# Feed forward of a gated block: output passes and transposes of the inner values, singly or in groups of two

## The chip, the cores and the metric

The kernel runs on one core of one Trainium2 chip. The metric is device microseconds from start to end of one execution, the median of several runs. The core has five engines with queues of their own: PE (TensorE: matmuls and transposes, with the weight loads shown apart as PEld), DVE (VectorE), ACT (ScalarE), POOL (GpSimd) and SP (SyncE, here only transfers). They meet through semaphores; each engine takes its own instructions strictly in the order in which they are written.

## The reference

The block is a cross attention (32 heads) with a gate, followed by a sparse feed forward with a gate. The change lies in the feed forward alone. Its mathematics, cut from the reference:

```python
xf = x.reshape(B * T, M)                      # 2048 rows of 512, after a layer norm
inter = xf @ c1_w.T @ c2_w.T                  # low rank selector, 1792 values a row
blk = inter.reshape(B * T, n_blocks, SPARSITY)  # 56 blocks of 32
idx = jnp.argmax(blk, axis=-1) + jnp.arange(0, INTER, SPARSITY)
h = jax.nn.relu(jnp.einsum('bkm,bm->bk', w1[idx], xf))
out = jnp.einsum('bk,bkm->bm', h, w2t[idx])
```

The result is x + tanh(g_ffn) * out.

## The kernel before

The first 1600 us of the program are the projections and the attention; they are not touched. The feed forward takes the rows in 16 tiles of 128 (`PAIRS` is 16; a tile is called j below). Instead of gathering, the kernel computes all 1792 inner values of a tile, multiplies them by a mask that keeps one in each block, turns them round, and multiplies by all of w2. Every product of full accuracy is three matmuls (`three`, lines 1345 to 1347), since each operand is held as a rounded part "hi" and a remainder "lo".

PE's steps, by the functions of the program:

- `hidden(t, k)`: inner values of tile t, column group k. Groups 0 to 2 have 512 columns, group 3 has 256. 12 matmuls a group.
- `selector(t, k)`: the selector values, one matmul a group (L1512).
- `transpose_h(t, k)`: turns round group k of the masked inner values (`h_picked`): 4 transposes of 128x128 for groups 0 to 2, 2 for group 3 (L1535).
- `output(t, k)`: adds group k to the tile's output: 12 matmuls for groups 0 to 2, 6 for group 3.
- `f_transpose_x(t)`: turns round the normalised input of tile t, 4 transposes (L1491), and `low_rank(u)`: the first selector product for two tiles, 12 matmuls of 256 columns. Both are done for two later tiles at once, in the tiles for which `prep` is true: j = 2, 4, 6, 8, 10, 12. These are called preparing tiles here.

PE writes tile j's stage as follows: output of tile j-1 and transposes of tile j in turns, then (preparing tiles) `low_rank`, then `hidden(j+1, k)` and `selector(j+2, k)` in turns.

What is transposed goes on in two steps: ACT copies the bank to `h_picked_t_hi` (`ht_hi`, L900), DVE computes `h_picked_t_lo` from the bank and that copy (`ht_lo`, L1241), and only then is the bank free. The two banks 4 and 5 serve all `transpose_h` groups in turn, and of the two `f_transpose_x` of a preparing tile the second: the list `ffn_uses` hands them out, in the order T0, T1, x(j+3), T2, T3 (T0 to T3 are the four groups of `transpose_h(j, .)`; x(j+2) goes to bank 7). So x(j+3) waits until `ht_lo` of T0 is done, T2 until `ht_lo` of T1 is, T3 until `xft_lo` of x(j+3) is. `output` accumulates in bank 6, `hidden` uses 0 and 1, `selector` 2 and 3.

DVE's own order, which is written by hand too, is for a tile j: `ht_lo(j,0)`, `ht_lo(j,1)`, in preparing tiles `fx_lo(j+2)` and `fx_lo(j+3)` (L1180), `block_rank(j+1)` (L1216, after POOL's `rank`, L701), `ht_lo(j,2)`, `first_max(j+1)` (L1222), `ht_lo(j,3)`, in preparing tiles `low_rank` (L1192 and L1194), `finish(j-1)` (L1246), then four times `pick_h(j+1,k)` (L1232) and `block_max(j+2,k)` (L1203), and at last `mark_max(j+2)` (L1211). `selector(j+2,0)` needs DVE's `low_rank`; `hidden(j+1,2)` needs bank 0, which `pick_h(j+1,0)` frees.

Of the kernel before, what the change touches and what calls it, by code (L numbers as in the profile page):

```python
# [112 lines left out]
def build(nc, x, ctx_t, bias, mask, gates, wq, wk, wv, wo, c1, c2, w1, w2, out):  # L113
# [17 lines left out]
    with ExitStack() as whole:  # L131
# [206 lines left out]
        def job_raw(r):  # L338
            _, is_v, i = JOBS[r]
            return vraw[i % 2] if is_v else kraw[i % 2]  # L340

        def job_dest(r):
            _, is_v, i = JOBS[r]
            return vw[i // 8][i % 2] if is_v else kw[i % 2]

        def job_raw_in(r):
            _, is_v, i = JOBS[r]
            return loaded(vraw_in if is_v else kraw_in, i)
# [59 lines left out]
        def split_done(n):  # L408
            return lo_sem[PIECES[n][5]], pieces_to(n, 5)

        def bank_free(use):
            b = f_before[use]
            if b is None:
                bk = f_bank[use]
                return (dve_s, dve_s, act_pt, act_pt, dve_clo, dve_clo, dve_wo, dve_wo)[bk], SLOTS
            if b[0] in ("x", "t", "out"):
                return {"x": dve_fx, "t": dve_ft, "out": dve_o}[b[0]], b[1] + 1
            return {"sel": act_i, "h": dve_hm, "ht": dve_hl}[b[0]], 4 * b[1] + b[2] + 1
# [924 lines left out]
        def _(pe):  # L1343
            def three(o, a, b, first_mm, last_mm, grouped=True):
                pe.matmul(o, a[0], b[0], start=first_mm, stop=False, skip_group_check=not grouped)  # L1345
                pe.matmul(o, a[0], b[1], start=False, stop=False, skip_group_check=not grouped)  # L1346
                return pe.matmul(o, a[1], b[0], start=False, stop=last_mm, skip_group_check=not grouped)  # L1347

            def hi_lo(ts_, *idx):
                return [t[idx] for t in ts_]  # L1350
# [136 lines left out]
            def f_transpose_x(t):  # L1487
                pe.wait_ge(*bank_free(("x", t)))
                pe.wait_ge(dve_xn, LN + t + 1)
                for c in range(CH):  # L1490
                    mm = pe.transpose(bank[f_bank[("x", t)]][:, c * P:(c + 1) * P],  # L1491
                                      fxn[t % 2][:, c * P:(c + 1) * P], ident[:, :])
                mm.then_inc(pe_x, 1)

            def low_rank(u):
                pe.wait_ge(*bank_free(("t", u)))
                pe.wait_ge(dve_fx, 2 * u + 2)
                if u == 0:
                    pe.wait_ge(*split_done(piece_no[("c1", 0)]))
                for c in range(CH):  # L1500
                    mm = three(bank[f_bank[("t", u)]][:, 0:FU], hi_lo(c1s, full, c, full),
                               hi_lo(xft[u % 2], full, c, full), c == 0, c == CH - 1)
                mm.then_inc(pe_t, 1)

            def selector(t, k):
                u, a = divmod(t, 2)
                pe.wait_ge(*bank_free(("sel", t, k)))
                pe.wait_ge(dve_ft, u + 1)
                if t == 0 and k == 0:
                    pe.wait_ge(*split_done(piece_no[("c2", 1)]))  # L1510
                c0, w = IB[k]
                pe.matmul(bank[f_bank[("sel", t, k)]][:, 0:w], ts[u % 2][:, a * P:(a + 1) * P],  # L1512
                          c2s[:, c0:c0 + w], start=True, stop=True).then_inc(pe_i, 1)

            def hidden(t, k):
                u, a = divmod(t, 2)
                c0, w = IB[k]
                pe.wait_ge(*bank_free(("h", t, k)))
                pe.wait_ge(dve_fx, t + 1)
                if t == 0:  # L1520
                    for n in range(c0 * CH // PIECE, (c0 + w) * CH // PIECE):
                        pe.wait_ge(*split_done(piece_no[("w1", n)]))
                for c in range(CH):
                    col = c0 * CH + c * w
                    mm = three(bank[f_bank[("h", t, k)]][:, 0:w],
                               hi_lo(xft[u % 2], full, c, slice(a * P, (a + 1) * P)),
                               hi_lo(w1s, full, slice(col, col + w)), c == 0, c == CH - 1)
                mm.then_inc(pe_h, 1)

            def transpose_h(t, k):  # L1530
                a, w = TGRP[k]
                pe.wait_ge(*bank_free(("ht", t, k)))
                pe.wait_ge(dve_hm, 4 * t + k + 1)
                for c in range(a, a + w):
                    mm = pe.transpose(bank[f_bank[("ht", t, k)]][:, (c - a) * P:(c - a + 1) * P],  # L1535
                                      hm[:, c * P:(c + 1) * P], ident[:, :])
                mm.then_inc(pe_ht, 1)

            def output(t, k):
                a, w = TGRP[k]  # L1540
                if k == 0:
                    pe.wait_ge(*bank_free(("out", t)))
                pe.wait_ge(dve_hl, 4 * t + k + 1)
                if t == 0:
                    for n in range(a // 2, (a + w + 1) // 2):
                        pe.wait_ge(*split_done(piece_no[("w2", n)]))
                for c in range(a, a + w):
                    o = (c % 2) * D
                    mm = three(bank[f_bank[("out", t)]][:, :], hi_lo(hmt, full, c, full),
                               hi_lo(w2s[c // 2], full, slice(o, o + D)), c == 0, c == IC - 1)  # L1550
                mm.then_inc(pe_ou, 1)
# [28 lines left out]
            hidden(0, 3)  # L1580
            for j in range(PAIRS):
                prep = j % 2 == 0 and j + 3 < PAIRS
                for k in range(4):
                    if j:
                        output(j - 1, k)
                    transpose_h(j, k)
                    if j and prep and k == 1:
                        f_transpose_x(j + 2)
                        f_transpose_x(j + 3)
                if prep:  # L1590
                    low_rank(j // 2 + 1)
                for k in range(4):
                    if j + 1 < PAIRS:
                        hidden(j + 1, k)
                    if j + 2 < PAIRS:
                        selector(j + 2, k)
# [58 lines left out]
```

## Time and profile before

| | us |
|---|---|
| median of 3 runs | 1982.55 |
| lowest and highest | 1980.14, 1984.99 |
| profiled execution | 1984.87 |
| its span | 1982.8 |
| PE busy in the span | 1932.2 |
| feed forward, from about 1600 to the end | 383 |

The span is the time from the first to the last instruction of the profiled execution; what lies around it is 2.07 us. A difference of about 0.2% (4 us) is what timed runs of this kernel tell from none. Start times in the rows are microseconds from the span's start. A matmul's duration overlaps the next one's, so the length of a stretch of PE's work is read from start to start.

### The profile page before, as it was taken

The page shows a single profiled execution, that of the slowest core. Times are in us where ns is not written, and L with a number is a line of the kernel's source. Part 1 is how long each engine was busy: PE and PEld are TensorE (multiplying, and loading weights), DVE is VectorE, ACT ScalarE, POOL GpSimd, SP SyncE. Part 2 cuts the span into 40 slices and gives each one's busy share as a digit, 9 for nine tenths or more (in the row PEclk, how much of TensorE's full clock was granted, in tenths as well). Part 3 has the DMA queues.
Part 4 walks back from the last instruction along what each step waited for, and adds up shares of the span by engine and source line. Part 5 has one row for each costly group of instructions (what it writes and reads, how often), then busy time and mean ns, then how long its engine had stood idle before and what let it go on. Part 6 is the DMA issues. An engine that isn't in the chain of part 4 may idle for free. (4 is left out here: it accounts for less than half of the span.)

```text
span 1982.8 us, 32380 instructions
## 1 busy us (share of the span) xinstructions
PE 1932.2 (97%) x12220; PEld 1675.9 (85%) x12220; DVE 1077.1 (54%) x1748; ACT 769.4 (39%) x1963; POOL 972.0 (49%) x772
## 2 busy tenths in 40 slices
PE   7999999999999999999899999999999869999999
PEld 5999988899988888888788888888888757888887
DVE  5343465333355553334366656765656676676773
ACT  3233333322233333333356555656565532222221
POOL 6766688766688787787322222223222342122110
PEclk8999999999999999999899999999999989999999
DMA  3555665554454554577597767888766331000000
GB/s 121 190 190 168 194 207 190 187 169 150 151 189 172 190 188 172 175 257 230 219 250 255 213 198 272 256 222 271 218 180 186 123 114 54 22 22 22 22 22 17
DMA packets 185578, 329.54 MB, mean 166 GB/s; under 512 B 11856, under 2 KB 118480, under 8 KB 176464
## 3 DMA queue, kind: packets, MB, share of 16 engines
q1 hardware_dynamic: 185424, 327.47, 51.6%
q8 instruction: 99, 1.62, 0.3%
q14 instruction: 55, 0.45, 0.1%
HBM read 214.17 MB, written 113.25 MB: 165 GB/s over the span
## 5 line engine op out<-in xcount | busy, mean ns | idle before, releaser
L1345 PE MATMUL bank<-tokens_hi,wkq_hi 128*128 128x512 f32 x896 | 352.4, 393 | 12.5 <-DVE tokens_lo L979 10.9
L1346 PE MATMUL bank<-tokens_lo,wkq_hi 128*128 128x512 f32 x896 | 351.1, 392 | 0.0
L1347 PE MATMUL bank<-tokens_hi,wkq_lo 128*128 128x512 f32 x896 | 351.1, 392 | 0.0
L664 POOL TENSOR_TENSOR wkq_lo<-raw_wkq,wkq_hi 128x768 fp32r<-128x768 f32 (+1 forms) x128 | 287.8, 2268 | 124.5 <-ACT wkq_hi L773 124.3
L1345 PE MATMUL bank<-wv_s_hi,tokens_hi 128*128 128x256 f32 x896 | 254.3, 284 | 1.5 <-POOL wv_s_lo L664 1.5
L1347 PE MATMUL bank<-wv_s_hi,tokens_lo 128*128 128x256 f32 x896 | 253.5, 283 | 0.0
L1346 PE MATMUL bank<-wv_s_lo,tokens_hi 128*128 128x256 f32 x896 | 253.5, 283 | 0.0
L687 POOL TENSOR_TENSOR bias_mask<-bias_in,mask_add 128x256 f32<-128x256 f32 x128 | 87.5, 684 | 308.2 <-DVE scores L1117 308.2
L1345 PE MATMUL bank<-wo_hi,attn_t_hi 128*128 128x512 f32 x512 | 213.7, 417 | 0.0
L1345 PEld LDWEIGHTS bank<-tokens_hi,wkq_hi 128*128 128x128 f32 x896 | 169.6, 189 | 50.4 <-DVE tokens_lo L979 11.9
L1347 PE MATMUL bank<-wo_hi,attn_t_lo 128*128 128x512 f32 x512 | 201.8, 394 | 0.0
L1346 PE MATMUL bank<-wo_lo,attn_t_hi 128*128 128x512 f32 x512 | 200.2, 391 | 0.0
L1347 PEld LDWEIGHTS bank<-tokens_hi,wkq_lo 128*128 128x128 f32 x896 | 169.5, 189 | 35.6
L1346 PEld LDWEIGHTS bank<-tokens_lo,wkq_hi 128*128 128x128 f32 x896 | 169.6, 189 | 34.7
L857 ACT ACTIVATE probs_t<-bank 64x256 f32<-64x256 f32 x256 | 96.7, 378 | 238.4 <-PE bank L1453 237.0
L791 ACT ACTIVATE p<-bank 128x512 f32<-128x512 f32 x96 | 57.4, 598 | 316.5 <-PE bank L1347 316.5
L844 ACT ACTIVATE exp<-scores,negmax 128x64 f32<-128x64 f32 x512 | 172.0, 337 | 10.8 <-DVE negmax L1121 7.5
L664 POOL TENSOR_TENSOR wv_s_lo<-raw_wv,wv_s_hi 128x1536 fp32r<-128x1536 f32 (+1 forms) x32 | 130.1, 4066 | 89.8 <-ACT wv_s_hi L773 89.8
L1345 PEld LDWEIGHTS bank<-wv_s_hi,tokens_hi 128*128 128x128 f32 x896 | 171.9, 192 | 2.1 <-POOL wv_s_lo L664 1.9
L999 DVE TENSOR_TENSOR c<-bank,u 128x512 f32<-128x512 f32 x96 | 66.4, 692 | 196.1 <-PE bank L1347 196.1
L1346 PEld LDWEIGHTS bank<-wv_s_lo,tokens_hi 128*128 128x128 f32 x896 | 172.0, 192 | 0.2
L1347 PEld LDWEIGHTS bank<-wv_s_hi,tokens_lo 128*128 128x128 f32 x896 | 171.9, 192 | 0.0
(115 smaller groups left out, 3910.9 us busy)
## 6 DMA issues: line engine op xcount, KB each, us to landing
k_t<-c SPq DMA_DIRECT2D x128, 256.0 KB, 2.4
v_by_head<-c SPq DMA_DIRECT2D x128, 256.0 KB, 2.2
q_t<-c SPq DMA_DIRECT2D x128, 256.0 KB, 2.2
kt<-k_t SPq DMA_DIRECT2D x16, 2048.0 KB, 8.2
qt<-q_t SPq DMA_DIRECT2D x16, 2048.0 KB, 13.0
v<-v_by_head SPq DMA_DIRECT2D x64, 512.0 KB, 9.0
raw_wkq<-in_wk SPq DMA_DIRECT2D x32, 512.0 KB, 3.9
raw_wv<-in_wv SPq DMA_DIRECT2D x16, 1024.0 KB, 6.0
```

The lines of the kernel that those rows point to most:

```text
L664: pool.tensor_tensor(lo, job_raw(r)[:, a:b, :], hi.bitcast(F32), ALU.subtract)\
L687: pool.tensor_tensor(bm[s % 2][:, :, :], bias_in[it % 2][:, p, :].rearrange("p (h k) -> p h k", h=HG), mask_add[:, tile, :].unsqueeze(1).b ...
L791: act.activation(e1[n % 2][:, :], bank[n % 2][:, :], ACT.Copy).then_inc(act_e1, 1)
L844: e = act.activation(ex[s % 2][:, h, :], sc[s % 2][:, h, :], ACT.Exp, bias=negmax[s % 2][:, h:h + 1], scale=1.0, accum_out=rsum[s % 2][:, ...
L857: e = act.activation(pt[s % 2][rows, :, :, h, :], bank[2 + s % 2][rows, 0:2 * P].rearrange("p (r b q) -> p r b q", r=2, b=2), ACT.Copy)
L999: dve.tensor_tensor(o_c["c12"][n % 2][:, :], bank[5 + n % 2][:, :], u2[:, :], ALU.add)\
L1345: pe.matmul(o, a[0], b[0], start=first_mm, stop=False, skip_group_check=not grouped)
L1346: pe.matmul(o, a[0], b[1], start=False, stop=False, skip_group_check=not grouped)
L1347: return pe.matmul(o, a[1], b[0], start=False, stop=last_mm, skip_group_check=not grouped)
```

## The change

PE's order is rewritten in the loop over tiles; no other engine's order changes, and the list of banks stays as it was. Where output group k and transpose group k took turns, two output groups are now written one after the other, then two transpose groups, and this twice per tile. The two `f_transpose_x` follow T1 as before. In tile 0, which has no output to compute, nothing moves.

```diff
-                for k in range(4):
+                for k in (0, 2):
                     if j:
                         output(j - 1, k)
+                        output(j - 1, k + 1)
                     transpose_h(j, k)
-                    if j and prep and k == 1:
+                    transpose_h(j, k + 1)
+                    if j and prep and k == 0:
                         f_transpose_x(j + 2)
                         f_transpose_x(j + 3)
```

The first place is PE in tile 4, a preparing tile, around T0. Before (`bank5<-ident` is T0, the bracket names the semaphores waited for; the second output group is 12 matmuls of pieces 2 and 3):

```order
8067 L1347 MATMUL bank6<-w2_hi_1_155,h_picked_t_lo_180 128x512
8068 L1535 MATMUL bank5<-ident_49,h_picked_151 128x128 [waits dve_ffn_hm,dve_ffn_ht_lo]
8069 L1535 MATMUL bank5<-ident_49,h_picked_151 128x128 x3
8070 L1345 MATMUL bank6<-w2_hi_2_157,h_picked_t_hi_179 128x512 [waits dve_ffn_ht_lo]
8071 L1346 MATMUL bank6<-w2_lo_2_158,h_picked_t_hi_179 128x512
...
8081 L1347 MATMUL bank6<-w2_hi_3_159,h_picked_t_lo_180 128x512
8082 L1535 MATMUL bank4<-ident_49,h_picked_151 128x128 [waits dve_ffn_hm,dve_ffn_ht_lo]
8083 L1535 MATMUL bank4<-ident_49,h_picked_151 128x128 x3
8084 L1491 MATMUL bank7<-ident_49,xn0_172 128x128 [waits dve_xn,dve_ffn_t]
8085 L1491 MATMUL bank7<-ident_49,xn0_172 128x128 x3
8086 L1491 MATMUL bank5<-ident_49,xn1_173 128x128 [waits dve_xn,dve_ffn_ht_lo]
```

And the same place after the change:

```order
8067 L1347 MATMUL bank6<-w2_hi_1_155,h_picked_t_lo_180 128x512
8068 L1345 MATMUL bank6<-w2_hi_2_157,h_picked_t_hi_179 128x512 [waits dve_ffn_ht_lo]
...
8079 L1347 MATMUL bank6<-w2_hi_3_159,h_picked_t_lo_180 128x512
8080 L1535 MATMUL bank5<-ident_49,h_picked_151 128x128 [waits dve_ffn_hm,dve_ffn_ht_lo]
8081 L1535 MATMUL bank5<-ident_49,h_picked_151 128x128 x3
8082 L1535 MATMUL bank4<-ident_49,h_picked_151 128x128 [waits dve_ffn_hm,dve_ffn_ht_lo]
8083 L1535 MATMUL bank4<-ident_49,h_picked_151 128x128 x3
8084 L1491 MATMUL bank7<-ident_49,xn0_172 128x128 [waits dve_xn,dve_ffn_t]
8085 L1491 MATMUL bank7<-ident_49,xn0_172 128x128 x3
8086 L1491 MATMUL bank5<-ident_49,xn1_173 128x128 [waits dve_xn,dve_ffn_ht_lo]
8087 L1491 MATMUL bank5<-ident_49,xn1_173 128x128 x3
```

T0 (bank 5) has moved down by 12 matmuls and stands right before T1. Between T0 and x(j+3), which writes the same bank and waits for DVE's reading of it, there were 12 matmuls and 8 transposes; now there are 8 transposes.

The second place is PE at the end of the same turn, around T2 (`bank4<-ident`), the third output group's end and the fourth group (piece 6). The piece of the difference:

```order
-L1535 MATMUL bank4<-ident_49,h_picked_151 128x128 [waits dve_ffn_hm,dve_ffn_ht_lo]
-L1535 MATMUL bank4<-ident_49,h_picked_151 128x128 x3
 L1345 MATMUL bank6<-w2_hi_6_165,h_picked_t_hi_179 128x512 [waits dve_ffn_ht_lo]
 L1346 MATMUL bank6<-w2_lo_6_166,h_picked_t_hi_179 128x512
...
 L1347 MATMUL bank6<-w2_hi_6_165,h_picked_t_lo_180 128x512
+L1535 MATMUL bank4<-ident_49,h_picked_151 128x128 [waits dve_ffn_hm,dve_ffn_ht_lo]
+L1535 MATMUL bank4<-ident_49,h_picked_151 128x128 x3
 L1535 MATMUL bank5<-ident_49,h_picked_151 128x128 [waits dve_ffn_hm,dve_ffn_xt_lo]
```

T2 has moved down by the 6 matmuls of the fourth output group; T3 and what follows keep their places in the row.

## Rows read from the trace of the kernel before

**Rows 1.** Page, busy time: engine, us, share of the span, instructions.
```profile
PE 1932.2 (97%) x12220; PEld 1675.9 (85%) x12220; DVE 1077.1 (54%) x1748; ACT 769.4 (39%) x1963; POOL 972.0 (49%) x772
```
**Rows 2.** Windows: stretch, length, busy time per engine, granted clock, DMA share, GB/s.
```profile
1600.00:1640.00 40.00, 25.47 (x125) 20.54 (x124) 27.80 (x33) 11.40 (x18) 19.10 (x10) 0.87 0.27 76
...
1720.00:1760.00 40.00, 40.00 (x208) 33.86 (x207) 27.90 (x38) 8.11 (x15) 5.38 (x5) 1.00 0.09 27
```
**Rows 3.** Waits, 1680 to 1960 us, the only one of PE's: total, times, longest.
```profile
PEld bank L1491 <- DVE h_picked_t_lo L1241: 0.8, 5, 0.2
```
**Rows 4.** Timeline, PE, tile 4: start, duration, line, instruction, count, [idle before].
```profile
1715.69 0.60 PE L1535 MATMUL bank<-ident,h_picked 128*128 128x128 f32 x4
1716.13 1.18 PE L1491 MATMUL bank<-ident,xn 128*128 128x128 f32 x8
1717.07 0.47 PE L1345 MATMUL bank<-w_hi,h_picked_t_hi 128*128 128x512 f32 x1
...
1719.90 0.60 PE L1535 MATMUL bank<-ident,h_picked 128*128 128x128 f32 x4
...
1721.72 0.38 PE L1535 MATMUL bank<-ident,h_picked 128*128 128x128 f32 x2
...
1726.11 0.39 PE L1512 MATMUL bank<-c_stacked,low_rank_stacked 128*128 128x512 f32 x1
1726.33 0.39 PE L1345 MATMUL bank<-w_hi,xft_hi 128*128 128x512 f32 x1
...
1729.05 0.39 PE L1512 MATMUL bank<-c_stacked,low_rank_stacked 128*128 128x512 f32 x1
```
**Rows 5.** Timeline, all engines, tile 4, around T1 and x(j+3).
```profile
1715.91 0.69 DVE L1241 TENSOR_TENSOR h_picked_t_lo<-bank,h_picked_t_hi 128x512 fp32r<-128x512 f32 x1
...
1716.33 0.60 ACT L900 ACTIVATE h_picked_t_hi<-bank 128x512 fp32r<-128x512 f32 x1 [2.59 <-PE bank L1535]
1716.65 0.42 PEld L1491 LDWEIGHTS bank<-ident,xn 128*128 128x128 f32 x4 [0.17 <-DVE h_picked_t_lo L1241]
...
1716.96 0.69 DVE L1241 TENSOR_TENSOR h_picked_t_lo<-bank,h_picked_t_hi 128x512 fp32r<-128x512 f32 x1 [0.36 <-ACT h_picked_t_hi L900]
```
**Rows 6.** Timeline, DVE, tile 4 and the tile after it.
```profile
1719.72 2.02 DVE L1216 TENSOR_REDUCE block_first<-is_max 128x56 bf16<-128x1792 bf16 x1 [0.88 <-POOL is_max L701]
1721.65 0.68 DVE L1241 TENSOR_TENSOR h_picked_t_lo<-bank,h_picked_t_hi 128x512 fp32r<-128x512 f32 x1
...
1724.96 0.43 DVE L1194 TENSOR_TENSOR low_rank_stacked<-bank,low_rank_stacked 64x256 fp32r<-64x256 f32 x1
...
1744.21 0.69 DVE L1241 TENSOR_TENSOR h_picked_t_lo<-bank,h_picked_t_hi 128x512 fp32r<-128x512 f32 x1 [0.58 <-ACT h_picked_t_hi L900]
...
1747.92 0.69 DVE L1232 SCALAR_TENSOR_TENSOR h_picked<-bank,first_max 128x512 f32<-128x512 f32 x1
```
**Rows 7.** Timeline, PE: T1, T2 of tile 5, `hidden(6,2)`, T1 of tile 6.
```profile
1739.74 0.60 PE L1535 MATMUL bank<-ident,h_picked 128*128 128x128 f32 x4
...
1742.94 0.60 PE L1535 MATMUL bank<-ident,h_picked 128*128 128x128 f32 x4
...
1750.89 0.39 PE L1345 MATMUL bank<-w_hi,xft_hi 128*128 128x512 f32 x1
...
1761.33 0.60 PE L1535 MATMUL bank<-ident,h_picked 128*128 128x128 f32 x4
```
**Rows 8.** Timeline, all engines, tile 1.
```profile
1645.40 0.47 PE L1345 MATMUL bank<-w_hi,h_picked_t_hi 128*128 128x512 f32 x1 [0.92 <-POOL w_lo L696]
...
1650.20 0.66 PE L1535 MATMUL bank<-ident,h_picked 128*128 128x128 f32 x4 [1.79 <-DVE h_picked_t_lo L1241]
...
1653.27 2.02 DVE L1216 TENSOR_REDUCE block_first<-is_max 128x56 bf16<-128x1792 bf16 x1 [2.53 <-POOL is_max L701]
...
1659.46 0.50 PE L1345 MATMUL bank<-w_hi,xft_hi 128*128 128x512 f32 x1 [1.10 <-DVE h_picked L1232]
1659.80 0.40 PE L1346 MATMUL bank<-w_lo,xft_hi 128*128 128x512 f32 x1
```

## The prediction

> **What bounds the kernel now.** I read the page's busy line first: PE is busy 97% of the span, every other engine at most 54% [rows 1]. That is an average, so the windows come next: from 1680 to 1960 us, which holds tiles 3 to 14, PE has no idle time at all at the full granted clock (one of seven such windows stands in the rows), while DVE is busy 28 of 40 us; only the first 80 us of the feed forward have holes [rows 2]. Third, the waits of that stretch: there is a single one that touches PE, five weight loads of `xn` (x(j+3)) held back by `h_picked_t_lo`, 0.8 us in all, at most 0.2 each [rows 3]. So the feed forward is a chain of PE instructions, and a change of order can pay only by what a turn between matmuls and transposes costs in itself, and can lose by every wait that comes into PE's queue. The one wait that exists is the very one whose cover the change takes away.
>
> **What a turn costs (the gain).** Four transposes followed by other transposes take 1716.13 - 1715.69 = 0.44 us [rows 4]. Twelve plain output-sized matmuls with nothing transposed between take 1729.05 - 1726.33 = 2.72 us [rows 4]. One transpose group and one output group in turns take 1742.94 - 1739.74 = 3.20 us [rows 7], so the turn costs 3.20 - 0.44 - 2.72 = 0.04 us. With six matmuls (half of 2.72 is 1.36) it is 1721.72 - 1719.90 - 0.44 - 1.36 = 0.02 us [rows 4]. I take 0.03 to 0.04; the bounds are 0.02 and 0.04. The change removes two turns in each of the tiles 1 to 15: 0.07 us a tile.
>
> The Trainium skill, "TensorE: Matmul & The Clock Gate", section "Part 2: What happens when you issue a matmul", says that the next weight load is pulled ahead of a running matmul, so that by its rule a turn should cost nothing. The rows show 0.02 to 0.04 us; by the rule the gain below would be 0 and the sum 6 x 0.94 = +5.6 instead of +4.7 us.
>
> **The first new wait: x(j+3), in the six preparing tiles.** x(j+3) writes the bank of T0, so it waits for ACT's copy and DVE's `ht_lo` of T0. Before, 12 matmuls lie between; now only T1 and x(j+2). I lay tile 4 out anew. T1 and all before it contain the same work less one turn, so T1 ends at 1716.13 - 0.03 = 1716.10, T1 starts at 1715.66 and T0 at 1715.22. From a group's start to ACT's copy it is 1716.33 - 1715.69 = 0.64 [rows 4, 5], from that to DVE's `ht_lo` 1716.96 - 1716.33 = 0.63, then 0.69 of work and 0.05 until the weight load of x(j+3) (the first `ht_lo` of the tile ends at 1715.91 + 0.69 = 1716.60, the load starts at 1716.65) [rows 5]. So x(j+3) can start at 1715.22 + 0.64 + 0.63 + 0.69 + 0.05 = 1717.23. DVE is free for that `ht_lo` from 1715.91, when it starts it today, and needs it at 1716.49. Without a wait x(j+3) would go at 1716.10 + 0.44 = 1716.54. The hold is 0.69.
>
> A hold costs PE a little more than its length. Today the twelve transposes from 1715.69 to 1717.07 take 1.38 us, and without a wait they would take eleven steps of 0.11 and 0.03 until the next matmul's start, 1.23 (the last transpose of a group is followed after 0.03: the four at 1719.90 to 1721.72 leave 1.47 for six matmuls, whose first two starts are 0.31 apart). So 0.15 are lost today, of which 0.09 is the hold (1716.65 less 1716.56) and 0.06 the refilling. New loss 0.69 + 0.06 = 0.75, old 0.15: 0.60 more per preparing tile.
>
> **The second new wait: the selector, in the same tiles.** What follows on PE comes 0.60 - 0.03 = 0.57 later. T2 in addition moves behind the fourth output group: 1719.90 + 0.57 + 1.36 = 1721.83 (rounded at the second turn). Its `ht_lo` can start at 1721.83 + 0.64 + 0.63 = 1723.10. Before, DVE ran it at 1721.65, right behind `block_rank` (1719.72, which waits for POOL and does not move); so DVE now idles 1.45 us. Behind that `ht_lo` stand, in DVE's own unchanged order, `first_max`, the last `ht_lo`, and the two instructions of `low_rank`, of which the second started 1724.96 - 1721.65 = 3.31 later and took 0.43 [rows 6]. Now it ends at 1723.10 + 3.31 + 0.43 = 1726.84, and the weight load of `selector(j+2,0)` can go 0.05 later, at 1726.89. Its natural place is 1726.11 + 0.57 - 0.03 (the second turn) + rounding = 1726.66 [rows 4]. The hold is 0.23. A matmul of 512 columns that was held loses more than the hold: at 1659.46 the next start follows after 0.34 instead of 0.23 [rows 8], 0.11 more. Cost 0.34. The cost is bounded below by 0 (if DVE ran the chain 0.25 us faster than laid out) and above by about 0.5.
>
> **Who else waits.** DVE comes out of this 1.45 us late. Only `finish` stands between `low_rank` and `pick_h(j+1,0)`, an instruction of some 0.8 us, so `pick_h` starts at about 1727.7 and is done at 1728.4; `hidden(j+1,2)` needs it behind the selector at 1729.05, now 0.9 later, so at about 1730. `pick_h(j+1,1)` waits for PE by 1.3 us in each tile, so DVE is in step again there. Nothing is passed on. In the other tiles T2's `ht_lo` moves from 1744.21 to 1744.21 + 1.36 - 0.07 = 1745.50, and `pick_h(6,0)` from 1747.92 to 1749.21, done at 1749.90 [rows 6]; `hidden(6,2)` starts at 1750.89 [rows 7] and loads its weights 0.22 before: 0.7 us of slack, no wait. T2 waits for T1's `ht_lo`, T3 for x(j+3)'s `xft_lo` and `output` for the previous tile's `ht_lo`: all lie microseconds back. `output(15, k)` at the end needs `ht_lo(15, k)`; T0 to T2 are done several us ahead.
>
> **Tile 1** has three stalls of its own: 0.92 for w2's last pieces (POOL), 1.79 for T0's `ht_lo` before T2, 1.10 for `pick_h` before `hidden(2,2)` [rows 8]. The middle one shrinks, since an output group now stands ahead of T2; but DVE's chain to `pick_h(2,0)` hangs on POOL's rank at 1653.27 and on the same `ht_lo`, not on PE, so `hidden(2,2)` starts at 1659.46 as before. Worth 0. Were it not caught there, at most 1.2 us would be won.
>
> **The sum**: six preparing tiles at 0.60 + 0.34 - 0.07 = 0.87 make 5.2. The eight others from 3 to 15 at -0.07 make -0.5. Tile 1 is 0. Together +4.7 us. The profiled execution, 1984.87, would become 1989.6; the median of the runs, which lies 2.32 below it, becomes 1982.55 + 4.7 = 1987.3. That is 0.24%, just over the 0.2% (4.0 us) that a measurement of this kernel tells from none.
>
> The Trainium skill, "Perfetto Trace Analysis", section "Matmuls", asks that independent groups rotate through banks so that the reading of one overlaps the matmuls of the next. By that rule the change is a loss wherever a bank is wanted again before about 1.9 us (0.64 + 0.63 + 0.69) are over; the new order does this for x(j+3) only, and the sum by the rule is the same first term.
>
> **Rivals.**
> (a) Only the first wait comes. The selector's hold rests on a difference of 0.23 between two chains of ten steps, each read to 0.01 to 0.05. Against it: each step is the same in five periods. Then 6 x (0.60 - 0.07) - 0.5 = +2.7: 1985.3, which counts as no change.
> (b) Faster: the transposes wait for nothing new, because the held x(j+3) is caught by work already queued, or a turn costs more than its start-to-start shows, and tile 1 keeps its 1.2 us. Price: 14 x 0.07 = -1.0, with tile 1 -2.2: 1980.4 to 1981.6. It decides if T0's `ht_lo` ended before 1716.54. Against: ACT and DVE need 1.96 us from T0's start, and T1 and x(j+2) give 0.88.
> (c) Slower by more: DVE's lateness is passed on. If `pick_h(j+1,0)` came another 1.45 us late in each of the eight other tiles, past their slack of 0.7, it would cost 8 x 0.75 = 6 us more: 1993. It decides when DVE's slack of 0.7 (other tiles) or about 1.7 (preparing ones) is used up. Against: the 1.3 us in which DVE waits for PE once per `pick_h`.
> (d) The change does not do what it says: the turns cost nothing and the waits stay hidden, 1982.5. Against: rows 4 and 7, and PE without a hole in the windows [rows 2].
>
> **Chances.** My forecast (both waits, +4 to +6) 0.62; (a) 0.22; (d) 0.04; (b) 0.06; (c) 0.06. A measurement's own spread (1980.14 to 1984.99 in three runs) adds 1 to 1.5 us to each, so some of the forecast's cases fall under 4.0 and some of (a)'s over it, and a little of (b)'s inside it: slower 0.60, same 0.34, faster 0.06. The range takes in the forecast and most of (a), with that spread: 1983.7 to 1990.3.
>
> **What would show it.** In the changed kernel's waits between 1680 and 1960 us: PE or PEld at L1491 held by `h_picked_t_lo` L1241 five times, 0.7 to 0.8 us each; the selector L1512 held by `low_rank_stacked` L1194, 0.2 to 0.3 each plus what the load shows; DVE idle 1.4 us before the third L1241 of a preparing tile. Two preparing tiles lie 45.64 us apart today (T1 at 1715.69 and 1761.33) [rows 4, 7]; they should lie 46.45 apart. In tile 1 the T2 wait should be 0.6 instead of 1.79 and `hidden(2,2)` should still start near 1659.5. I am wrong if the selector is not held, if ACT's or DVE's copies are quicker when two groups come together, or if PE's time between the waits is not the plain sum.

## The result and the profile after

The changed kernel is slower, as forecast.

| | before | after |
|---|---|---|
| median | 1981.52 us (8 runs) | 1987.73 us (8 runs) |
| lowest and highest | 1979.61, 1984.99 | 1986.22, 1990.62 |
| ratio, 95% interval | 1 | 1.0031 [1.0021, 1.0041] |
| span of the profiled execution | 1982.8 | 1985.8 |

The medians differ by 6.2 us; the interval, 4.2 to 8.1 us, still holds the forecast's 4.7. The two profiled executions differ by 3.0 us only. That they differ by less comes from outside the feed forward: windows over the first 40 us (length, busy PE, PEld, DVE, ACT, POOL, granted clock, DMA share, GB/s; before, then after) show a mean clock of 0.79 and of 0.87, in code that is the same.

```profile
0.00:40.00 40.00, 25.84 (x85) 20.38 (x86) 21.94 (x19) 14.53 (x16) 24.00 (x55) 0.79 0.34 113
```
```profile
0.00:40.00 40.00, 26.90 (x101) 21.35 (x102) 23.60 (x21) 15.91 (x17) 26.99 (x57) 0.87 0.37 125
```

At the first selector of the feed forward the changed kernel's execution is 4.19 us ahead, so every comparison below starts there. The first selector and the last instruction, before and then after (timelines of PE and DVE):

```profile
1592.33 0.61 PE L1512 MATMUL bank<-c_stacked,low_rank_stacked 128*128 128x512 f32 x2
...
1979.62 0.75 DVE L1246 SCALAR_TENSOR_TENSOR x_tile<-bank,gate_tanh,x_tile 128x512 f32<-128x512 f32 x1 [8.04 <-PE bank L1347]
```
```profile
1588.14 0.61 PE L1512 MATMUL bank<-c_stacked,low_rank_stacked 128*128 128x512 f32 x2
...
1982.53 0.75 DVE L1246 SCALAR_TENSOR_TENSOR x_tile<-bank,gate_tanh,x_tile 128x512 f32<-128x512 f32 x1 [7.47 <-PE bank L1347]
```

That is 387.29 us before and 394.39 after: the feed forward is 7.1 us longer. I call this length the stretch, and compare it with before's. The medians can't be told apart below a few us. A place in the stretch can be read to a few hundredths, but it moves by more from one execution to the next: where `hidden(2,2)` waits for DVE's unchanged chain it starts 67.06 to 67.47 us into the stretch in eight executions, so that a difference of under 0.4 us between two stretches says little by itself. The amounts per tile further on repeat within about 0.05 us.

Where it went is told by the waits of PE from 1680 to 1965 us (who waits, for whom, total, times, longest), which answer to [rows 3]:

```profile
PEld bank L1491 <- DVE h_picked_t_lo L1241: 3.9, 5, 0.8
...
PEld bank L1512 <- issue: 2.8, 5, 0.6
PE bank L1491 <- DVE h_picked_t_lo L1241: 2.7, 5, 0.5
...
PE bank L1512 <- DVE low_rank_stacked L1194: 0.9, 5, 0.2
```

Where there was one kind of wait of at most 0.2 us there are two: x(j+3) for the reading of T0's bank, and the selector for DVE's `low_rank`, each five times (the sixth preparing tile, tile 2, lies ahead of this window). Both are in tile 4's timeline, which answers to [rows 4, 5, 6]:

```profile
1713.65 1.04 PE L1535 MATMUL bank<-ident,h_picked 128*128 128x128 f32 x8
1714.53 0.60 PE L1491 MATMUL bank<-ident,xn 128*128 128x128 f32 x4
1715.67 0.66 PE L1491 MATMUL bank<-ident,xn 128*128 128x128 f32 x4 [0.54 <-DVE h_picked_t_lo L1241]
1716.08 0.48 PE L1345 MATMUL bank<-w_hi,h_picked_t_hi 128*128 128x512 f32 x1
...
1720.26 0.82 PE L1535 MATMUL bank<-ident,h_picked 128*128 128x128 f32 x6
...
1725.43 0.47 PE L1512 MATMUL bank<-c_stacked,low_rank_stacked 128*128 128x512 f32 x1 [0.17 <-DVE low_rank_stacked L1194]
```
```profile
1718.14 2.02 DVE L1216 TENSOR_REDUCE block_first<-is_max 128x56 bf16<-128x1792 bf16 x1 [0.46 <-POOL is_max L701]
1721.53 0.69 DVE L1241 TENSOR_TENSOR h_picked_t_lo<-bank,h_picked_t_hi 128x512 fp32r<-128x512 f32 x1 [1.37 <-ACT h_picked_t_hi L900]
...
1724.85 0.43 DVE L1194 TENSOR_TENSOR low_rank_stacked<-bank,low_rank_stacked 64x256 fp32r<-64x256 f32 x1
```

T0 and T1 are the first row, x(j+2) the second; x(j+3) starts 1715.67 - 1714.53 = 1.14 us after it instead of 0.44. On DVE the third `ht_lo` is now preceded by an idle 1.37 us, `low_rank` ends at 1725.28, and the selector, whose weight load goes at 1725.39, is the next to start on PE:

```profile
1725.39 0.19 PEld L1512 LDWEIGHTS bank<-c_stacked,low_rank_stacked 128*128 128x128 f32 x1 [0.57 <-issue]
```

("issue" says that the profile names no releaser for this weight load; the matmul behind it names `low_rank`.)

The third place was not forecast. It is tile 1, at the wait for `pick_h` before `hidden(2,2)`. After the change (compare the last row but one of [rows 8], 1.10 us):

```profile
1655.35 0.50 PE L1345 MATMUL bank<-w_hi,xft_hi 128*128 128x512 f32 x1 [2.27 <-DVE h_picked L1232]
```

Windows over the 12 matmuls of that `hidden(2,2)`, before and after (the granted clock is the figure behind POOL's busy time):

```profile
1659.46:1662.33 2.87, 2.87 (x12) 2.36 (x13) 1.73 (x3) 0.00 (x0) 0.00 (x0) 1.00 0.42 126
```
```profile
1655.35:1659.79 4.44, 4.44 (x13) 3.50 (x13) 1.72 (x3) 0.00 (x0) 0.00 (x0) 0.62 0.35 118
```

The same matmuls take 4.44 us instead of 2.87. The matmul ahead of which PE stood idle for 2.27 us is at the same place of the stretch as before (1655.35 - 1588.14 = 67.21 against 1659.46 - 1592.33 = 67.13), but behind it the clock was at 1.2 instead of 2.4 GHz for part of the window, a loss of 1.57 us.

So the 7.1 us are 0.1 up to `hidden(2,2)`, 1.6 there, 6 preparing tiles, and eight others. One preparing tile costs about 1.0: in tile 4 the stretch grows by 0.59 up to the third output group's start, gives 0.03 back at the second removed turn and grows by 0.43 at the selector. The others bring 0.07 each on average (0.05 to 0.08), as forecast: 0.1 + 1.6 + 6.0 - 0.6 = 7.1.

### The profile page after: what moved, and what is told of

Its sections match the earlier page's. It is cut to its first block and busy times, and to the rows that moved or that the text cites. A ratio compares the mean times of both kernels' runs of the same rounds, so it can differ in the third digit from the quotient of the medians.

```text
span 1985.8 us, 32380 instructions
## 1 busy us (share of the span) xinstructions
PE 1932.2 (97%) x12220; PEld 1676.9 (84%) x12220; DVE 1075.3 (54%) x1748; ACT 766.8 (39%) x1963; POOL 971.9 (49%) x772
```

## The experiments

All runs compare with the kernel before on the same chip. The theory to be tested has three parts: the hold of x(j+3) comes from pairing T0 with T1, the hold of the selector from moving T2 behind the fourth output group through DVE's order, and the slow clock in tile 1 from the longer hole ahead of `hidden(2,2)`. The stretch of a run is given as its difference from before's 387.29 us.

### One pair at a time

```diff
-                for k in range(4):
-                    if j:
-                        output(j - 1, k)
-                    transpose_h(j, k)
-                    if j and prep and k == 1:
+                for ks in ((0, 1), (2,), (3,)):
+                    if j:
+                        for k in ks:
+                            output(j - 1, k)
+                    for k in ks:
+                        transpose_h(j, k)
+                    if j and prep and ks[-1] == 1:
                         f_transpose_x(j + 2)
                         f_transpose_x(j + 3)
```

This is the first run's edit of the kernel before; the second run has `((0,), (1,), (2, 3))` in its place.

> Only the first two groups are paired (output 0, output 1, T0, T1, both x), the last two take turns as before. Theory (two waits and a hole in tile 1): x(j+3) is held as in the changed kernel, about 0.57 us per preparing tile; T2 moves by no more than that, so DVE's chain to low_rank ends in time (about 1725.5 against a natural weight load at 1726.4, in tile 4's terms of the kernel before) and the selector is not held; tile 1 keeps its old hole of 1.1 us before hidden(2,2) and its full clock. Sum 6 x 0.57 - 8 x 0.03 = +3.2 us against the kernel before. Rival (the selector is late because DVE is late anyway once x is late): the selector is held too, +5.5.

Measured: 1985.14 against 1982.08 us, ratio 1.0016 [1.0007, 1.0025]; stretch +3.3 (+3.2 expected). PE's only waits between 1680 and 1965 us:

```profile
PEld bank L1491 <- DVE h_picked_t_lo L1241: 3.9, 5, 0.8
PE bank L1491 <- DVE h_picked_t_lo L1241: 2.7, 5, 0.5
```

x(j+3) is held exactly as in the changed kernel, the selector not at all. The rival falls: x being late does not by itself make the selector late.

> Only the last two groups are paired (output 2, output 3, T2, T3), the first two take turns as before. Theory: no new hold of x(j+3) (it keeps its 0.15 us); T2 moves by 1.36 us and with it DVE's third h_picked_t_lo, first_max and low_rank, so the selector is held and costs 0.40 to 0.43 us per preparing tile, 6 x 0.43 - 14 x 0.03 = +2.2. In tile 1 T2 stands behind output 3 as in the changed kernel, so the hole before hidden(2,2) grows to 2.3 us and the clock falls behind it to half for 3.4 us, 1.4 more: +3.6. Rival (the clock's fall has nothing to do with the hole): +2.2, with full clock after tile 1.

Measured: 1986.79 against 1982.08 us, ratio 1.0023 [1.0014, 1.0032]; stretch +4.4. The waits of the same window:

```profile
PEld bank L1512 <- issue: 2.8, 5, 0.6
PE bank L1512 <- DVE low_rank_stacked L1194: 0.8, 5, 0.2
```

Now only the selector is held, by the same amounts as in the changed kernel, and the hole in tile 1 is 2.30 us, with a mean clock of 0.93 in the window from 1640 to 1664 us. The rival (full clock) falls. The stretch is 0.8 above the sum expected: 0.3 are there when `hidden(2,2)` starts, 0.2 are the clock's loss of 1.6 instead of 1.4, and the rest is spread over the preparing tiles.

### Tile 1 apart

The same loop, with this head in the third run:

```diff
-                for k in range(4):
+                for ks in ((0,), (1,), (2,), (3,)) if j == 1 else ((0, 1), (2, 3)):
```

and this in the fourth:

```diff
-                for k in range(4):
+                for ks in ((0, 1), (2, 3)) if j == 1 else ((0,), (1,), (2,), (3,)):
```

> The changed kernel, but with the old order in tile 1 alone. Theory (the larger hole before hidden(2,2) lets the clock fall): hole 1.1 us, full clock from there on, 1.4 us less than the changed kernel, so +5.4 against the kernel before. Rival (the fall was a chance of that one execution): half clock at the same place again, or no difference in the times, +6.5.

Measured: 1987.14 against 1982.08 us, ratio 1.0024 [1.0015, 1.0033]; stretch +5.5. The hole is 1.07 us and the clock full; of the 7.1 us, 1.6 are gone. The medians don't separate this kernel from the changed one (1987.73 in its own comparison); the traces do. Ten of the eleven times of this run lie between 1985.14 and 1988.59 us, the eleventh is 3729.62.

> The kernel before, with the new order in tile 1 alone. Theory: hidden(2,2) waits for DVE's pick_h as before, but from 1.2 us earlier, so the hole is 2.3 us; the clock falls to half for 3.4 us behind it and the kernel loses 1.4 us, with the rest as before: +1.4. Rival (as predicted before the change was run): the hole costs nothing because it only moves, 0.0 to -0.2.

Measured: 1983.61 against 1982.08 us, ratio 1.0010 [1.0001, 1.0019]; stretch +1.6. Here nothing else is changed. The hole, and the windows from 1640 to 1664 us of this run and of the third:

```profile
1656.29 0.50 PE L1345 MATMUL bank<-w_hi,xft_hi 128*128 128x512 f32 x1 [2.30 <-DVE h_picked L1232]
```
```profile
1640.00:1664.00 24.00, 20.61 (x95) 16.33 (x94) 15.41 (x20) 5.08 (x9) 6.06 (x4) 0.93 0.12 40
```
```profile
1640.00:1664.00 24.00, 20.54 (x99) 16.45 (x98) 16.28 (x22) 5.46 (x11) 7.61 (x6) 1.00 0.11 41
```

0.93 against 1.00: a hole that "only moves" is not free. The rival, which was my own step in the prediction, falls.

### What holds the selector

Fifth run, x(j+3) behind the third output group (PE):

```diff
+                        for k in ks:
+                            output(j - 1, k)
+                            if move and k == 2:
+                                f_transpose_x(j + 3)
...
+                    if move and ks[-1] == 1:
+                        f_transpose_x(j + 2)
```

(`move` is `j and prep`, the groups are those of the changed kernel.)

> The changed kernel, but x(j+3) is written behind the third output group, so that T0's bank is free long before. Theory (the selector hangs on DVE's chain, and DVE's fx_lo(j+3), which stands ahead of block_rank in DVE's order, now comes at 1720.5 instead of 1718.2 in tile 4's terms, so block_rank starts 1.4 us late): the hold of x(j+3) is gone (-0.57 us and the 0.15 of before), but the selector's hold grows from 0.25 to about 0.9 us and costs 1.1 instead of 0.43; per preparing tile +0.9 against the kernel before, the same as the changed kernel. Sum 6 x 0.9 - 0.6 + 1.4 for tile 1 = +6.3. Rival (the two waits are independent): 6 x (0.43 - 0.18) - 0.6 + 1.4 = +2.3.

Measured: 1988.37 against 1981.72 us, ratio 1.0038 [1.0024, 1.0051]; stretch +6.9, 0.6 above the expected sum (a preparing tile costs 1.0 instead of 0.9). The first wait is gone, but the kernel is as slow as the changed one. The waits from 1682 to 1960 us, and DVE in tile 4:

```profile
PEld bank L1512 <- issue: 6.3, 5, 1.3
PE bank L1512 <- DVE low_rank_stacked L1194: 4.3, 5, 0.9
```
```profile
1719.43 0.69 DVE L1180 TENSOR_TENSOR xft_lo<-bank,xft_hi 128x512 fp32r<-128x512 f32 x1 [2.20 <-ACT xft_hi L883]
1720.04 2.01 DVE L1216 TENSOR_REDUCE block_first<-is_max 128x56 bf16<-128x1792 bf16 x1
1721.97 0.68 DVE L1241 TENSOR_TENSOR h_picked_t_lo<-bank,h_picked_t_hi 128x512 fp32r<-128x512 f32 x1
...
1725.28 0.43 DVE L1194 TENSOR_TENSOR low_rank_stacked<-bank,low_rank_stacked 64x256 fp32r<-64x256 f32 x1
```

`fx_lo(j+3)` waits 2.20 us for the later x, and `block_rank` behind it in DVE's order starts late: the selector's hold rises from 0.17 to 0.9 us and takes back what the first wait gave up. The two waits are not independent; the rival (+2.3) falls.

Sixth run, PE as changed, DVE's order in preparing tiles edited:

```diff
                     ht_lo(j, 2)
+                    if prep:
+                        ht_lo(j, 3)
+                        low_rank(j // 2 + 1)
                     if nxt:
                         first_max(j + 1)
-                    ht_lo(j, 3)
-                    if prep:
-                        low_rank(j // 2 + 1)
+                    if not prep:
+                        ht_lo(j, 3)
```

> The changed kernel on PE; on DVE, in preparing tiles, the last h_picked_t_lo and low_rank stand ahead of first_max instead of behind it (2.0 us). Theory: low_rank ends at about 1725.1 in tile 4's terms, the selector is not held, and x(j+3) still is: 6 x 0.54 - 0.6 + 1.4 = +4.1 to +4.5, 2.6 less than the changed kernel. Rival (first_max and pick_h, now 0.8 us later, hold hidden(j+1,2) instead): no gain or a wait L1345 held by h_picked L1232.

Measured: 1986.32 against 1981.72 us, ratio 1.0028 [1.0017, 1.0039]; stretch +4.35, that is 2.75 less than the changed kernel (2.6 expected). PE's waits from 1682 to 1960 us hold only x(j+3):

```profile
PEld bank L1493 <- DVE h_picked_t_lo L1241: 3.9, 5, 0.8
PE bank L1493 <- DVE h_picked_t_lo L1241: 2.7, 5, 0.5
```

It was `first_max`, 2.0 us of DVE, ahead of `low_rank`. (The lines are two further down in this kernel.) The rival's wait at `hidden(j+1,2)` does not appear.

### All three taken away

Seventh run: the edits of the third, fifth and sixth together. Eighth run: these, and in tile 0 on DVE

```diff
                     if j == 0:
+                        if k == 3:
+                            mark_max(2)
                         for m in range(n, n + (2 if k == 0 else 1)):
                             split(m)
```

with `mark_max(j + 2)` at the loop's end left out for j = 0.

> Grouped turns with all three causes taken away: x(j+3) behind the third output group, low_rank ahead of first_max on DVE, the old order in tile 1. Theory: no PE wait from 1680 us on, each preparing tile 0.15 to 0.18 shorter than in the kernel before (its small wait gone, two turns less, one more), the others 0.07: -1.1 - 0.6 = -1.6 against the kernel before, a difference that only the trace can show. Rival (grouping costs something beyond these three): 0 or above.

Measured: 1979.46 against 1981.72 us, ratio 0.9991 [0.9982, 1.0000]; stretch -1.1 where -1.6 was expected. PE has no wait at all from 1682 us on. With the waits gone the grouping does give its turns back: a preparing tile is 0.14 us shorter than before, another tile 0.07. Of the 0.5 us missing, 0.2 are there when tile 2's stage starts, and 0.2 are the preparing tiles' 0.14 where 0.15 to 0.18 were laid out. In this execution the clock fell too, behind T2's hole in tile 1:

```profile
1646.76 0.70 PE L1537 MATMUL bank<-ident,h_picked 128*128 128x128 f32 x4 [2.01 <-DVE h_picked_t_lo L1241]
1647.17 0.72 PE L1347 MATMUL bank<-w_hi,h_picked_t_hi 128*128 128x512 f32 x1
1647.69 0.63 PE L1348 MATMUL bank<-w_lo,h_picked_t_hi 128*128 128x512 f32 x1
```

It cost little there, because what came late ran into the next hole, the one before `hidden(2,2)` (1.07 us in the third run), and filled it. `hidden(2,2)` starts at 67.49 us of the stretch without any hole, against 67.16 in the third run, which has the same order in tile 1: of the clock's loss 0.3 us were left there.

> As e7, and in tile 0 DVE's mark_max(2) is done ahead of the split of w2's last piece instead of behind it. Theory: POOL's rank and with it DVE's chain to pick_h(2,0) start 3 to 4 us earlier, T2 of tile 1 waits at most 0.2 us instead of 1.8, hidden(2,2) is not held (1.1 before): about 3 us more, -4.6 against the kernel before (0.9977). Rival (the split of w2's last piece then holds output(0,3), or the clock falls elsewhere): -1.6 or above.

Measured: 1978.63 against 1981.72 us, ratio 0.9990 [0.9982, 0.9999]; stretch -2.8 where -4.6 was expected. This is the fastest kernel of the study by its trace, and its interval lies just below 1. The hole before T2 is 0.53 us, but the one before `hidden(2,2)` is still 0.85, not 0. The reason is in DVE's and POOL's rows:

```profile
1640.44 3.57 DVE L1211 TENSOR_TENSOR is_max<-selector,block_max 128x1792 bf16<-128x1792 f32 x1
```
```profile
1639.76 2.37 POOL L696 TENSOR_TENSOR w_lo<-raw,w_hi 128x1024 fp32r<-128x1024 f32 x1 [4.66 <-ACT w_hi L876]
1644.09 4.53 POOL L701 TENSOR_TENSOR is_max<-is_max,earlier_is_larger 128x1792 bf16<-128x1792 bf16 x1 [1.96 <-DVE is_max L1211]
```

Moved up, `mark_max` lies beside POOL's split of a w2 piece and takes 3.57 us instead of 2.02; POOL's rank then lies beside DVE's own split and takes 4.53 instead of 3.6. The chain starts 3.9 us earlier in the stretch, 2.5 are lost so, and `hidden(2,2)` starts 1.4 earlier.

### The hole and the clock

The same edit on the changed kernel and on the kernel before, to change the hole without touching PE's order:

> The changed kernel on PE, untouched; only DVE's mark_max(2) in tile 0 stands ahead of the split of w2's last piece, as in the last run. Theory (it is the hole's length that lets the clock fall): DVE's chain to pick_h(2,0) ends 1.4 us earlier, the hole before hidden(2,2) shrinks from 2.3 to about 0.9 us, the clock stays full, and the kernel is 1.4 + 1.4 = 2.8 us faster than the changed one, +3.9 to +4.3 against the kernel before. Rival (the paired order in tile 1 itself, not the hole, lets the clock fall): half clock for 3.4 us again, only 1.4 us gained, +5.7.

Measured: stretch +3.9, inside the expected range. The hole is 1.33 us (0.9 expected) and the clock stays full:

```profile
1654.34 0.50 PE L1347 MATMUL bank<-w_hi,xft_hi 128*128 128x512 f32 x1 [1.33 <-DVE h_picked L1232]
```
```profile
1640.00:1664.00 24.00, 21.98 (x109) 17.77 (x108) 19.29 (x24) 5.08 (x9) 7.93 (x6) 1.00 0.10 33
```

PE's order in tile 1 is that of the changed kernel, so in this execution the order by itself did not let the clock fall. The medians do not bear this out: 1986.92 against 1981.46 us, ratio 1.0031 [1.0020, 1.0043], 7 runs from 1985.14 to 1991.96. That is +5.5, nearer to the rival's +5.7 than to the theory's +4.3, though the interval (+4.0 to +8.5) leaves room for both. The profiled execution is the shortest of the seven. The mean granted clock of the seven goes from 0.987 to 0.991, which does not say where in the program it was lower, so whether the clock stayed full in tile 1 of the other six stays open.

> The kernel before with the same one edit on DVE. Theory: the hole before hidden(2,2) goes from 1.1 us to about 0, the one before T2 of tile 1 from 1.8 to about 0.5 us, the rest is unchanged: -1.4 us. Rival (the hole moves on to a later place): 0.

Measured: 1981.05 against 1981.46 us, ratio 0.9997 [0.9988, 1.0007]; stretch -1.2, and `hidden(2,2)` starts 1.35 us earlier in it. T2's hole is 0.53 us, the one before `hidden(2,2)` 0.87 (1.10 before): the first shrank as expected and the second by little, since PE arrives earlier too; the gain is the one expected all the same.

The holes of tile 1 in all twelve profiled executions, by what PE's clock did right behind them:

| executions | longest hole in tile 1 | clock behind it |
|---|---|---|
| changed kernel, second, fourth, fifth, sixth run | 2.27 to 2.30, before `hidden(2,2)` | fell for 3.4 us |
| seventh run | 2.01, before T2 | fell for 3.4 us |
| kernel before, first, third run | 1.79 to 1.80, before T2 | full |
| eighth, ninth, tenth run | at most 1.33 | full |

In tile 1, then, the length of the hole and the clock go together in all twelve. It is not shown that length alone decides: only one execution has a hole between 1.80 and 2.27 us, and it lies at another place. And outside tile 1 the same traces go both ways at about 1.8 us. In tile 0 of all twelve, PE stands idle for 1.87 or 1.88 us before T3, and the clock stays full behind it. The kernel before there, T3 and a window over what follows:

```profile
1624.17 0.44 PE L1535 MATMUL bank<-ident,h_picked 128*128 128x128 f32 x2 [1.88 <-DVE h_picked_t_lo L1241]
```
```profile
1624.20:1630.00 5.80, 5.80 (x33) 5.08 (x34) 4.80 (x6) 2.28 (x3) 5.80 (x2) 1.00 0.10 18
```

In the first 40 us of the same execution an idle time of 1.83 us ends at 31.26 us, and the clock is at half from 31.74 on, for 6.8 us:

```profile
29.43:31.26 1.83, 0.00 (x1) 0.00 (x1) 1.83 (x3) 1.46 (x2) 0.29 (x1) 1.00 0.00 0
```
```profile
31.74:38.57 6.83, 5.96 (x15) 4.17 (x14) 2.14 (x4) 0.00 (x0) 4.51 (x5) 0.50 0.11 41
```

What else the clock goes by stays open.

## Why the prediction was right, and where it was short

**That PE's row of instructions is the bound, and a turn costs 0.03 to 0.04 us**: right. The eight other tiles gave 0.07 us each on average, and the seventh run, with the waits away, shows the gain alone.

**The first new wait** (0.69 of hold, 0.60 of loss, 0.57 net): right. The trace shows weight loads held by 0.77 us after the previous load and 0.54 between matmuls, 5 times; the first run, which has this wait alone, grows by 0.57 us with each preparing tile and the tile behind it together. In the changed kernel x(j+3) of tiles 4 and 6 start 46.54 us apart (1715.67 and 1762.21), where 46.45 was forecast for two preparing tiles.

**The second new wait** (0.23 of hold, cost 0.34): right in its chain, mis-sized in the last steps of its sum. T2's `ht_lo` was preceded by 1.37 us of idle time where 1.45 was laid out, and `low_rank` ended 0.19 us after the selector's natural start (1725.28 against 1724.86 + 0.23 = 1725.09), where the layout has 1726.84 - 1726.66 = 0.18. But from DVE's end to the weight load it took 1725.39 - 1725.28 = 0.11 us and not 0.05, and from the load to the matmul another 0.04, which the sum left out: it set the time of the load against the natural start of the matmul. So the selector started 0.34 us late instead of 0.23. The refilling was smaller than its term, about 0.09 instead of 0.11 (the next start follows after 0.31 instead of 0.23). Together the loss is 0.43. 6 x 0.09 = 0.5 us of the sum were missed here; 0.2 more are small differences in the first term.

**Nobody else waits**: right. No other PE wait exists from 1680 to 1965 us; DVE's lateness ends at the second `pick_h`, as laid out: in tile 4's stage it is preceded by 1.35 us of waiting for PE.

**Tile 1 worth 0**: this step failed. Its mechanism was right as far as it went: `hidden(2,2)` starts at 67.2 us of the stretch in both kernels. What it left out is what PE does behind the hole. PE came to it 1.2 us earlier (the hole before T2 was 0.47 instead of 1.79; 0.6 was forecast) and so stood idle for 2.27 instead of 1.10 us, and the clock fell behind it: 1.57 us. The fourth run has this term alone (+1.6), the third is without it, and in the ninth's trace it is gone with a shorter hole in the same order. That the fall went with the long hole is shown; by what rule the clock falls is not.

**The sum**: 4.7 forecast; the stretch gives 7.1, the medians 6.2. The forecast time, 1987.3, lies closer to the measured 1987.73 than the sum does, and that is luck: it starts from before's median of three runs, 1982.55, while that of eight is 1981.52. The terms are 6 x 1.0 instead of 6 x 0.87, plus 1.6 instead of 0; -0.6 instead of -0.5 for the others. Of the rivals, (a) was refuted by the selector's five holds, (b) by x(j+3)'s five, (c) by PE having no wait for `pick_h` behind tile 1, and (d) by the two holds together.

## What to carry to other kernels

Where one engine is without a gap, a new order of its work is priced by two lists: what a turn costs from start to start (here 0.03 us, next to nothing), and, for each buffer, the time from the last write to the next one against the readers' chain (here 1.96 us from T0 to a free bank, with 0.88 us of work left between). Follow a moved instruction into the next engines' fixed orders too: the selector was held because `first_max` stood between T2's reader and `low_rank`. Which wait is loosened matters: to loosen that of x(j+3) alone gave 0.2 us, since the selector's grew in its place, while to loosen the selector's alone gave 2.75. And a hole whose end is fixed by another engine is not free to grow: what runs behind it may run at half the clock.

## What the runs showed of the hardware

An idle time of PE of 2.0 to 2.3 us in tile 1, with one or two shorter ones in the 15 us before it, was followed by a fall of the granted clock from 2.4 to 1.2 GHz for 3.4 us in six executions of six; where the longest was 1.8 us or less the clock stayed full, in six of six. Elsewhere in the same traces an idle time of 1.83 us was followed by a fall and one of 1.88 was not, so this is no rule of length alone. Only these twelve profiled executions are known. Behind the fall, the matmuls of 512 columns started 0.42 us apart instead of 0.23.

Where a DVE and a POOL instruction that read SBUF lay side by side, the one that started second took longer: `mark_max`, begun 0.7 us behind POOL's split, took 3.57 us instead of 2.02, and POOL's rank, begun 0.2 us behind DVE's split, took 4.53 instead of 3.6. The split that had started first kept its time in both cases (2.37 and 1.21 us). The ninth and tenth run, with the same edit, show the same within 0.01 us.

The Trainium skill, "SBUF — State Buffer", section "SBUF: two separate sides", describes a port pair which the two share as an exclusive lock, also for a DVE instruction with two inputs in SBUF. The rows fit: DVE lost 1.55 us where 1.7 of POOL's instruction were left, and POOL lost 0.9 where 1.05 of DVE's were. This explanation was not tested apart.
